# Layer 1 of a four-layer image kernel: the second pair of query projections moved from the second to the third quarter of a unit

## The reference, cut to what matters

```python
up = xs @ W_up.T
x_m, z = (up[..., :INNER], up[..., INNER:])
x_conv = conv_b + sum((xp[:, k:k + S, :] * conv_w[:, 0, k] for k in range(K)))
x_act = jax.nn.silu(x_conv)
q = jnp.einsum('bsnd,nod->bsno', xa, Wq).reshape(B, S, INNER)
...
ig = (gate_in @ W_i.T + b_i).transpose(0, 2, 1)
fg = (gate_in @ W_f.T + b_f).transpose(0, 2, 1)
lc = jnp.cumsum(jax.nn.log_sigmoid(fg), axis=-1)
...
D = jnp.exp(logD - m)
Cmat = jnp.einsum('bhid,bhjd->bhij', qh, kh) * D
norm = jnp.maximum(jnp.abs(Cmat.sum(-1, keepdims=True)), jnp.exp(-m))
h_cell = jnp.einsum('bhij,bhjd->bhid', Cmat / (norm + EPS), vh)
hn = (h_cell - mu) / jnp.sqrt(var + LN_EPS)
h = (hn * norm_w + skip * x_act) * jax.nn.silu(z)
out = h @ W_down.T
```

## Time and profile before

| | before |
|---|---|
| median of 3 runs | 3328.1 us |
| lowest, highest | 3321.17, 3329.22 us |
| the profiled execution | 3324.22 us |
| its span in the profile | 3322.4 us |
| busy: TensorE, VectorE, ScalarE, GpSimd | 3016.2, 2143.1, 1994.1, 1133.1 us |
| mean granted TensorE clock | 0.955 |

### The profile page before, as it was taken

One profiled execution on the slowest core, in us unless ns is written; L12 is line 12 of the kernel. 1 busy time (PEld: TensorE's weight loads), 2 busy tenths in 40 slices (PEclk: granted clock), 3 DMA queues, 4 the chain that ended last, 5 costly groups with the idle time before them and its releaser, 6 DMA issues. The chain is left out here.

```text
span 3322.4 us, 103102 instructions
## 1 busy us (share of the span) xinstructions
PE 3016.2 (91%) x43288; PEld 1669.9 (50%) x43288; DVE 2143.1 (65%) x5155; ACT 1994.1 (60%) x4348; POOL 1133.1 (34%) x1441
## 2 busy tenths in 40 slices
PE   6999999999996999999999987989997788888886
PEld 3333333333323656556565555667765455555554
DVE  5887878878864676767667653555454466666664
ACT  2767667676664555564555533555554677777774
POOL 3343433433421322222222211323222455555553
PEclk8999999999997999999999998999998899999997
DMA  6877877778672233233322223555543233333332
GB/s 196 164 175 144 182 170 163 167 171 179 143 180 85 62 85 84 68 87 87 87 69 82 64 68 125 175 169 159 172 144 118 73 90 118 116 117 121 114 104 78
DMA packets 298892, 411.55 MB, mean 124 GB/s; under 512 B 39328, under 2 KB 255808, under 8 KB 277824
## 3 DMA queue, kind: packets, MB, share of 16 engines
q1 hardware_dynamic: 276720, 272.65, 27.3%
q0 software_dynamic: 18000, 131.08, 19.7%
q10 hardware_dynamic: 3712, 1.23, 0.1%
HBM read 219.47 MB, written 53.81 MB: 82 GB/s over the span
## 5 line engine op out<-in xcount | busy, mean ns | idle before, releaser
L859 ACT ACTIVATE l_sizes<-l_probs 128x2048 f32<-128x2048 f32 x256 | 487.0, 1908 | 301.3 <-DVE l_probs L800 293.6
L1936 POOL TENSOR_TENSOR l_logits<-l_logits,l_inv 128x400 f32<-128x400 f32 x256 | 245.0, 958 | 743.4 <-DVE l_inv L1915 737.7
L1929 ACT ACTIVATE l_logits<-l_logits,l_low 128x100 f32<-128x100 f32 x1024 | 372.6, 366 | 208.8 <-DVE l_low L1909 208.3
L301 PE MATMUL l_psum<-shared_x,shared_space 128*128 128x512 f32 x896 | 411.8, 605 | 12.7 <-DVE l_row_var L1482 11.6
L800 DVE TENSOR_TENSOR l_probs<-l_psum,l_decay 128x1024 f32<-128x1024 f32 x256 | 299.7, 1218 | 85.0 <-PE l_psum L674 74.0
L800 DVE TENSOR_TENSOR l_probs<-l_psum,shared_space 128x1024 f32<-128x1024 f32 x256 | 300.3, 1218 | 75.1 <-PE l_psum L674 74.5
L674 PE MATMUL l_psum<-l_qk 32*128 32x512 f32 x2048 | 340.5, 644 | 6.6 <-DVE l_qk L759 3.3
L967 POOL DMA_DIRECT2D l_sizes<-l_sizes x125 | 108.6, 869 | 537.3 <-ACT l_sizes L859 525.3
L1726 POOL TENSOR_TENSOR shared_space<-shared_space,l_causal 128x1024 f32<-128x1024 f32 x64 | 152.8, 2388 | 372.2 <-DVE l_x_act L1424 225.6
L689 PE MATMUL l_psum<-l_probs,shared_x 128*32 128x512 f32 x2048 | 270.6, 600 | 0.2
L301 PEld LDWEIGHTS l_psum<-shared_x,shared_space 128*128 128x128 f32 x896 | 163.8, 192 | 200.3 <-issue 194.4
(11 more groups left out here) (245 smaller groups left out, 5817.8 us busy)
## 6 DMA issues: line engine op xcount, KB each, us to landing
l_sizes<-l_sizes POOLq DMA_DIRECT2D x125, 1024.0 KB, 7.6
l_V_windows<-v_image SPq DMA_DIRECT2D x512, 100.0 KB
l_V_windows<-v_padded SPq DMA_DIRECT2D x512, 100.0 KB
shared_space<-rows_c SPq DMA_DIRECT2D x64, 512.0 KB, 5.9
shared_x<-y SPq DMA_DIRECT2D x24, 1024.0 KB, 5.6
y<-l_res SPq DMA_DIRECT2D x31, 512.0 KB, 3.4
l_e_everywhere<-rows_e SPq DMA_DIRECT2D x112, 128.0 KB, 5.6
shared_x<-x SPq DMA_DIRECT2D x8, 1024.0 KB, 12.2
```

What stands on the lines that cost most here:

```text
L301: i = nc.tensor.matmul(out, w[:, k, m * P:(m + 1) * P], act[:, k, n0:n1], start=(k == 0), stop=(k == tiles - 1))
L859: nc.scalar.activation(sizes[:, slot(N), :, :], probs[:, N % 2, :, :], ACT.Abs).then_inc(sized, 1)
L1929: nc.scalar.activation(e, e, ACT.Exp, scale=-1.0, bias=self.low[:, N % 4, i:i + 1], accum_out=self.total[:, N % 4, i:i + 1]).then_inc(self ...
L1936: nc.gpsimd.tensor_tensor(p, p, self.inv[:, N % 4, :].unsqueeze(2).to_broadcast([P, STEP, NKEY]), ALU.mult).then_inc(self.p_ready, 1)
```

## The change

In the filler list the second pair of queries, `("q", n, 1)`, goes from the end of quarter 1 to quarter 2, behind the two `r` and ahead of `tok`. ScalarE's copy of that pair out of PSUM goes with it: from quarter 1, behind the copy of the first pair, to quarter 2, ahead of `token_values`. `layer1_order` is built from the same list, so the ring's regions and what each fill waits for change too. Nothing is computed more or less.

```diff
--- before.py
+++ after.py
@@ -1006,7 +1006,7 @@
 
     n, f = u + 1, u - 1
     ups = [("up", k, m) for k in layer1_ups(u) for m in range(2)]
-    names = {0: [("z", f, 0), ("z", f, 1), ("g", n)], 1: [("fi", n), ("q", n, 0), ("q", n, 1)], 2: [("r", f, 0), ("r", f, 1), ("tok", n)],
+    names = {0: [("z", f, 0), ("z", f, 1), ("g", n)], 1: [("fi", n), ("q", n, 0)], 2: [("r", f, 0), ("r", f, 1), ("q", n, 1), ("tok", n)],
              3: ups + [("down", f)]}[t]
     names = [name for name in names if 0 <= name[1] < UNITS]
     if t == 0 and u % 2 == 0 and 0 < u // 2 + 1 <= B:
@@ -1695,8 +1695,8 @@
                     if t == 1 and 0 <= n < UNITS:
                         log_sigmoid(n)
                         copy_queries(n, 0)
+                    if t == 2 and 0 <= n < UNITS:
                         copy_queries(n, 1)
-                    if t == 2 and 0 <= n < UNITS:
                         token_values(n)
                         row_exps(n)
                     if t == 3:
```

## The result

| | before | after |
|---|---|---|
| median, lowest to highest | 3321.17 (3312.65 to 3329.22), 7 runs | 3351.09 (3334.64 to 3369.32), 7 runs |
| ratio after to before, 95% interval | | 1.0094 [1.0067, 1.012] |
| the profiled execution, its span | 3324.22, 3322.4 | 3348.03, 3346.2 |
| mean granted clock | 0.955 | 0.952 |
| TensorE busy | 3016.2 | 3028.0 |

What follows compares the result with a forecast made beforehand. TensorE was taken as nearly always busy, with unit length set by `up`'s start, which waits for a fade held by masks. 0.2 + 6.9 + 0.6 = +7.7 on 3324.2 gave 3332 us, range 3319 to 3343.

Steps and rivals of the forecast that it cites:

- the length of a unit is the start of `up` plus a constant: Layer 1, units 1 to 13: after `up` starts, 41.5 us remain in odd units and 43.6 in even ones.
- forecast 4.42: Quarter 2: `r` starts 4.42 us after zero (start of scan L1451) instead of 4.85, with TensorE idle 1.76 instead of 0.42.
- the copy, the stores and L1403 hidden, L1497: ScalarE's 1.0 us copy, SyncE's store some 1.3 later, and VectorE's L1403 and L1497 would not delay TensorE.
- forecast 7.37: Quarter 2: `tok` starts 7.37 us after zero instead of 6.04, +1.33, behind the moved pair's 1.76.
- the masks in their places: GpSimd's masks don't move; the second starts between 12.04 and 13.63 us after zero.
- forecast at 206.0: Thirteen starts of `up` without the clock: eight at 16.38 held by the second mask, five at 15.0, against 205.8 before.
- The clock: Quarter 2: nine of thirteen units fall to 1.2 GHz as before; only five free units pay, 2.0 us each: +6.9.
- the forecast's 12.74: Quarter 2: VectorE's fade starts 12.74 us after zero instead of 11.41; in eight of thirteen units the second mask starts earlier.
- the third rival: Quarter 2: the clock stays low from the moved pair through `weigh`; three units give 11 us more, 3343; chance 0.22.
- The +0.2: Thirteen starts of `up`, 206.0 against 205.8 us: the 1.33 is mostly unpaid because in many units TensorE already stands there.
- The rule on the clock: Rival, quarter 2: a dense pair between weak stretches stops the clock falling; sum 0.2 + 0.6, 3325 us; chance 0.2.
- the base: The sum was added to one profiled execution, 3324.2 us; the median of three runs was 3.9 above it.

Runs made afterwards that it cites:

- Kernel 1: Changed kernel plus two extra 128x512 matmuls, used by nobody, in the idle gap ahead of `r` in quarter 2: 3318.74 us, 0.9991 to before.
- kernel 3: Kernel before with `weigh` issued ahead of `tok` in quarter 2, nothing added: 3301.86 us, ratio 0.9942 to before.
- first and second profile: One profiled execution each from the original and the repeat runs, both kernels unchanged; thirteen units: before 758.3 and 747.3 us, changed 776.3 and 782.3.
- 2: Changed kernel with `weigh` issued ahead of `tok` in quarter 2: 3338.57 us, ratio 1.0062 to before.
- 8: Changed kernel with the moved query pair behind `tok` instead of ahead of it: 3353.5 us, ratio 1.0095 to before.
- Kernel 5: Kernel 1 with GpSimd's second mask made to wait until `ud` of quarter 2 has been taken: 3311.44 us, ratio 0.9958 to before.
- kernel 4: Changed kernel with the moved pair ahead of the two `r` in quarter 2 instead of behind them: 3309.87 us, ratio 0.9966 to before.
- 11: Changed kernel with the pair ahead of `r` and `weigh` ahead of `tok`: 3312.35 us, ratio 0.9937 to before.

## Why the prediction was wrong

**Right, and measured:** the length of a unit is the start of `up` plus a constant, after the change too (60.40 - 16.77 = 43.63 in unit 2, 59.21 - 17.74 = 41.47 in unit 3). `ud` ahead of zero, the idle time moved ahead of `s`; `r` at 4.29 and 4.35 for a forecast 4.42; the copy, the stores and L1403 hidden, L1497 in odd units only; `tok` at 7.27 in an odd unit without a fall (forecast 7.37); the masks in their places (12.07 to 13.22). Without the clock the thirteen starts of `up` were forecast at 206.0. Kernel 1, where the clock stays up, has 755.36 less the constants, 552.5: 202.9.

**The step that failed** is the one headed "The clock": "Where the second mask holds the fade anyway, one short fall is covered. In the five free units a fall delays the fade into the mask", and the 2.0 x 5 x 9/13 = 6.9 us that came of it. The count of falls was nearly right (ten and eleven for nine). The price was not: from kernel 1 to the changed kernel the units grow by 21.0 us in one profile and 26.9 in the other. Set apart by even and odd units, in us:

| | before, no fall (3) | before, first and second profile | changed, no fall (1) | changed, first and second profile |
|---|---|---|---|---|
| six even units | 345.5 | 360.8, 347.8 | 361.0 | 363.8, 361.6 |
| seven odd units | 387.8 | 397.5, 399.5 | 394.4 | 412.6, 420.7 |

The cover is real, but only in even units: there falls cost 2.8 and 0.6 us. In odd ones they cost 18.2 and 26.3. Kernel 1 shows why. With the clock up an odd unit has its fade at 12.57, ahead of the second mask in six of seven, where the forecast's 12.74 had put four of them (5, 7, 9 and 11) behind it. And a fall there costs more than 2.0: against the 56.0 us of an odd unit that nothing holds, 2.1 and 2.5 where it is short, 3.2 to 4.8 where it is long (`up` at 17.7 or 19.3 instead of 14.5). In five and seven units of the thirteen it is long; before the change, when the gap ahead of `r` was 0.42 and not 1.62, in three and four.

The long fall is the third rival, "the clock falls ahead of the moved pair and stays down", which the text priced at 3.7 us a unit and put into three units because three had shown a long fall before. Its place is what kernels 1, 2 and 8 show, and its price was about right. The size was off in how many units it takes. The text had the ground for it, "1.76 of pure idleness ahead of `r` is new", and left the forecast's own count and price as they were.

**What the sum hid.** The +0.2 ("The 1.33 is not paid in full") sets a changed kernel without falls against a kernel before with nine. In the kernel before, falls cost 25 and 14 us (758.3 and 747.3 against the 733.3 of kernel 3, whose units are as long as those of before that did not fall). With no fall on either side the move costs 22 us in these units, 755.4 against 733.3, and 15.4 of them lie in the six even ones: `tok` is 1.55 later there, the fade goes from 11.45 to 13.02, and in kernel 1 that is behind the start of the second mask in all six. Kernel 5 puts the second mask's part at 10 us and leaves 12 for TensorE's own later L1348.

So of the mean 26.5 us between the kernels some 22 are the move itself, and the falls, 24 us now and 19.5 before, add only 4 to 5. That kernel 1 comes out level with before is no sign that the order is free; the old order's falls cost about what the new order does. A short fall makes L1348 late by 1.2 to 1.7 us in both kernels, whether it meets `tok` and `weigh` or the pair; what differs is what the mask covers and how long the fall lasts.

**The rule on the clock**, that activity releases the throttle (the Trainium skill, TensorE: Matmul & The Clock Gate, "What's actually happening"), was weighed as a rival: a dense pair between two weak stretches would keep the clock up. The runs agree with the rule and not with what was made of it. Dense work in the gap keeps the clock up (kernel 1; in kernel 4 for the pair itself, while six units fall behind `tok`), and so does dense work that parts two weak pieces with little idleness ahead (3 and 11). Behind the gap it comes too late (2 and 8).

**A second error** is the base. The sum was set on one execution, and another has 11.0 us less in the same units. The forecast missed the measured median by 19 us with this base, which was the higher of the two; on the lower one it would have missed by more. Against the profiled execution (3348.0) it missed by 16: 11 in the units, and the rest in the part behind them, which grew by 6.6 us for a forecast 0.6. Two executions of one kernel differ there by nearly as much.

## What to carry to other kernels

Where the matrix engine is the bound and its clock falls after weak stretches, first ask what the old order and the new one take with the clock up in both; a profile of before that has falls in it makes a move look free that isn't. Then ask of a moved block which side of the gap it lands on: ahead of the wait it fills it, behind it it runs at half speed. A fall is covered only where another wait, here a mask, already holds the unit for longer. Small or few-row matmuls that nobody needs soon belong behind a dense block that is ready, not in a row behind a wait (here, `weigh` ahead of `tok` was worth 0.6% for nothing). And a kernel whose clock falls by chance needs the profiles of several executions before a sum is set on one of them.

## What the runs showed of the hardware

In even units `tok` of the changed kernel starts at 7.65 or later, 0.4 behind odd ones, though 0.06 was forecast. VectorE's L1410, which reads two SBUF tiles, now starts earlier and meets the first half of GpSimd's group norm (VectorE's row of unit 2 first, then GpSimd's of two instructions of 1.4):

```profile
1208.00 1.06 DVE L1410 TENSOR_TENSOR l_q_weighted<-l_q,l_e_everywhere 128x512 f32<-128x512 f32 x1
```

```profile
1207.33 2.80 POOL L448 TENSOR_SCALAR shared_x<-shared_x,shared_gn_negmean,shared_gn_rstd 128x1024 f32<-128x1024 f32 x2
```

It takes 1.06 us instead of 0.68 and ends 0.33 behind the first norm instruction (1207.33 + 1.40); it is 1.06 or 1.07 in all six even units. In the kernel before, where it started 5.87 after zero (1209.21) and not 5.31, with the norm at 4.73 and not 4.64, it took 0.68. It looks like the fade and the mask over again: the later start left only the tail of the first norm instruction in its way. The Trainium skill (SBUF — State Buffer, "Who interferes with whom") says that whichever starts first keeps the port; these rows fit it, but no run here moved the norm to try it. So 0.4 us of what VectorE gained in quarter 1 was lost again in even units. The hold of the fade by a mask is firmer: in every unit of both kernels where a mask still ran when the fade began, the fade ended 0.29 us behind it, and with the second mask moved away (kernel 5) it took 0.43 in each even unit.
